# A decoder kernel of two attention calls: the rows of narrow layers' next item normalised by ScalarE, the order of wide layers changed

## The reference, cut to what matters

```python
x = x + _L0_attn_ref(_layernorm(x), ...)      # "window": keys within 32 positions
x = x + _L0_xattn_ref(ctx, ctx, _layernorm(x), padding_mask, ...)   # "cross_pad": 77 context keys
x = x + _L0_ffn_ref(_layernorm(x), ...)       # mixture of 8 experts, the best 2
x = x + _L1_attn_ref(_layernorm(x), ...)      # "causal"
x = x + _L1_xattn_ref(_layernorm(x), ctx, ctx, mask, ...)           # "cross_mask": 77 context keys
x = x + _L1_ffn_ref(_layernorm(x), ...)       # quantised, gated
```

## Time and profile before

| | |
|---|---|
| time, median of 3 runs | 2198.09 us (2197.56 to 2198.1) |
| the profiled execution | 2189.82 us, its span 2188.2 us |
| PE busy | 1992.9 us (91%) |
| DVE busy | 1245.5 us (57%) |
| ACT busy | 965.0 us (44%) |
| POOL busy | 688.6 us (31%) |
| first attention call, in the span | about 0 to 655 us |
| experts | about 655 to 1205 us |
| second attention call | about 1205 to 1851 us |
| feed-forward | about 1856 to 2188 us |

### The profile page before, as it was taken

How to read it: one execution, slowest core, us unless ns; L and a number is a source line. 1 busy time by engine, 2 the same in 40 slices (tenths; PEclk the granted TensorE clock), 3 DMA queues, 4 the chain that set the end, 5 groups by cost and what they waited for, 6 DMA issues and landing times. The chain is left out here.

```text
span 2188.2 us, 51471 instructions
## 1 busy us (share of the span) xinstructions
PE 1992.9 (91%) x17362; PEld 1531.9 (70%) x17362; DVE 1245.5 (57%) x5443; ACT 965.0 (44%) x1849; POOL 688.6 (31%) x1254
## 2 busy tenths in 40 slices
PE   7999998999967999999999799999988887999869
PEld 5777776666646999999998577777666664444357
DVE  5778885566641101111115688888777775459964
ACT  3455555666632333333333255555545553357400
POOL 3566665245561000000001545553422220013400
PEclk9999999999978999999999899999999998999989
DMA  7333332233319999999995644333233321000023
GB/s 216 108 106 108 103 122 86 89 106 111 112 68 359 376 339 346 337 347 336 347 335 190 186 127 135 122 125 108 83 99 97 95 92 43 0 0 1 0 58 96
DMA packets 209108, 334.50 MB, mean 153 GB/s; under 512 B 59453, under 2 KB 193250, under 8 KB 199874
## 3 DMA queue, kind: packets, MB, share of 16 engines
q1 hardware_dynamic: 194482, 301.82, 39.6%
q0 software_dynamic: 9552, 26.10, 3.9%
q10 hardware_dynamic: 4928, 4.72, 0.6%
HBM read 193.74 MB, written 28.05 MB: 101 GB/s over the span
## 5 line engine op out<-in xcount | busy, mean ns | idle before, releaser
L1913 ACT ACTIVATE moe_h<-moe_h_ps,moe_weights 128x128 f32<-128x128 f32 x424 | 132.8, 364 | 254.3 <-PE moe_h_ps L1885 226.0
L2344 PE MATMUL ffn_prod_ps<-x_sb,ffn_weights 128*128 128x512 f32 x480 | 210.9, 599 | 9.7 <-ACT ffn_sig_q L2330 7.0
L1251 ACT ACTIVATE causal_prob<-causal_ps 128x768 f32<-128x768 f32 (+1 forms) x192 | 168.7, 879 | 113.2 <-PE causal_ps L1500 111.8
L1945 DVE TENSOR_TENSOR moe_y<-moe_y_ps,moe_weights 128x256 f32<-128x256 f32 x53 | 22.5, 425 | 328.1 <-PE moe_y_ps L1895 328.1
L1885 PE MATMUL moe_h_ps<-moe_h,moe_weights 128*128 128x128 f32 x1696 | 198.0, 275 | 0.0
L1832 POOL DMA_DIRECT2D moe_y_dram<-moe_y x71 | 39.4, 555 | 494.6 <-DVE moe_y L1945 494.6
L1885 PEld LDWEIGHTS moe_h_ps<-moe_h,moe_weights 128*128 128x128 f32 x1696 | 193.6, 192 | 0.1
L2344 PEld LDWEIGHTS ffn_prod_ps<-x_sb,ffn_weights 128*128 128x128 f32 x480 | 91.0, 192 | 127.2 <-issue 110.2
L984 DVE CUSTOM_DVE_ANT_0 causal_masked<-causal_ps,causal_causal_mask 128x256 bf16<-128x256 f32 (+1 forms) x512 | 152.4, 354 | 45.2 <-PE causal_ps L1466 43.5
L984 DVE CUSTOM_DVE_ANT_0 window_masked<-window_ps,window_window_mask 128x160 bf16<-128x160 f32 x512 | 135.3, 320 | 60.4 <-PE window_ps L1466 57.8
L1251 ACT ACTIVATE window_prob<-window_ps 128x640 f32<-128x640 f32 x128 | 90.0, 703 | 97.7 <-PE window_ps L1500 96.2
(11 more groups left out here) (376 smaller groups left out, 4675.8 us busy)
## 6 DMA issues: line engine op xcount, KB each, us to landing
moe_weights<-moe_w_in SPq DMA_DIRECT2D x53, 2180.0 KB, 9.0
q_pair<-parts SPq DMA_DIRECT2D x512, 128.0 KB
parts<-moe_w_in SPq DMA_DIRECT2D x18, 2180.0 KB, 8.9
k_pair<-parts SPq DMA_DIRECT2D x256, 128.0 KB
k_pair<-parts SPq DMA_DIRECT2D x256, 38.5 KB
moe_rows<-moe_slots_dram SPq DMA_DIRECT2D x71, 128.0 KB, 3.1
moe_y_dram<-moe_y POOLq DMA_DIRECT2D x71, 128.0 KB, 3.4
x_before_ffn_dram<-x_sb SPq DMA_DIRECT2D x16, 256.0 KB, 2.2
```

The source lines that it names most:

```text
L1251: nc.scalar.activation(out, src, ACT.Exp).then_inc(expd, 1)
L1913: nc.scalar.activation(out[:, f, :], psum[:, f // 2, (f % 2) * TM:(f % 2) * TM + TM], ACT.Gelu, bias=bias[:, f:f + 1]).then_inc(done, 1)
L2344: op = nc.tensor.matmul(prod_ps[:, slot, f, :].rearrange("p (b t) -> p b t", b=2), w[:, k, at:at + P], x_cols(n // GROUPS, k), start=(k == ...
```

## The change

Two names are added: wide(ref), true where the layer at lag 2 has two pairs, and by_scalar(ref), true where there is a next item and the layer at lag 2 is narrow.

1. POOL's layernorm makes also a shift, -mean x rstd, by two more 128x2 operations with a semaphore wait before each, for every item; `scaled_by` is raised behind them. It waits for `normed` of t - 1 first.
2. Where by_scalar(ref) holds, DVE's normalise in slot 7 is left out. ACT makes the rows by two ACTIVATEs with scale rstd and bias shift at the end of slot 4, ahead of the copy of v and of max_rows; it waits for `scaled_by` and `xT_mm`.
3. In wide steps PE's turn of xn goes ahead of shifted(0). max_out for the first half of the maxima goes from slot 4 to slot 7, ahead of the output projection, and ACT's max_rows from slot 5 to slot 7. PE's transposes of the output wait for one maximum fewer.
4. The second half of the tail's turn goes to bank 0, like the first, and waits for ACT's copy of the first instead of for `q_lo` and `added`; ACT's copy of it stands at the end of slot 4 and no longer waits for `v_ev`.
5. In DVE's slot 2 the low part of q goes ahead of the last layernorm's statistics.

```diff
@@ attention()
         ln = layernorm_tiles(sb)
+        shift = ln["var_eps"]
+        negative = sb("negative", [P, ST], F32)
+        def wide(ref):
+            return active(ref, 2) and layer_at(ref, 2).pairs == 2
+        def by_scalar(ref):
+            return active(ref, -1) and active(ref, 2) and not wide(ref)
@@ POOL
                 def layernorm(t, ref):
                     pool.wait_ge(stat, t + 1)
-                    inverse_deviation(nc, pool, ln, ref % 2, pool_chain, 1 + t, scaled_by)
+                    par = ref % 2
+                    wait(pool, normed, t - 1)
+                    inverse_deviation(nc, pool, ln, par, pool_chain, 1 + t, deviated)
+                    pool.wait_ge(deviated, t + 1)
+                    nc.gpsimd.tensor_tensor(shift[par][:], ln["mv"][par][:, :, 0], ln["rstd"][par][:], ALU.mult).then_inc(shift_one, 1)
+                    pool.wait_ge(shift_one, t + 1)
+                    nc.gpsimd.tensor_tensor(shift[par][:], shift[par][:], negative[:], ALU.mult).then_inc(scaled_by, 1)
@@ DVE
+                        if i == 2 and active(ref, 0):
+                            low_part(q_parts[par], q_ps, layer_at(ref).bq, q_hi, q_lo, t, S)
                         if i == 2 and in_tail(ref, 4):
...
-                        if i == 2 and active(ref, 0):
-                            low_part(q_parts[par], q_ps, layer_at(ref).bq, q_hi, q_lo, t, S)
@@
-                        if i == 7 and active(ref, -1):
+                        if i == 7 and active(ref, -1) and not by_scalar(ref):
                             dve.wait_ge(scaled_by, t + 2)
@@ ACT
+                def normal_rows(t, ref):
+                    par = ref % 2
+                    act.wait_ge(scaled_by, t + 1)
+                    act.wait_ge(xT_mm, t - 1)
+                    gate(act, act_passed)
+                    for s in range(ST):
+                        op = nc.scalar.activation(xn[par][:, s, :], in_x(t, ref)(t, s), ACT.Identity, bias=shift[par][:, s:s + 1],
+                                                  scale=ln["rstd"][par][:, s:s + 1])
+                    op.then_inc(normed, 1)
@@
-                    if k == 1 and active(ref, 0):
-                        act.wait_ge(v_ev, t + 1)
...
-                    nc.scalar.activation(out, bank(k)[:, S:2 * S], ACT.Copy).then_inc(last_ev, 1)
+                    nc.scalar.activation(out, bank(0)[:, S:2 * S], ACT.Copy).then_inc(last_ev, 1)
@@
-                        if i == 5 and in_tail(ref, 5):
-                            keep_turned(t, ref, 1)
-                        if i == 5 and active(ref, 1):
+                        if i == 5 and active(ref, 1) and not wide(ref):
                             max_rows(t, 1, 0)
@@
+                        if i == 4 and by_scalar(ref):
+                            normal_rows(t + 1, ref + 1)
+                        if i == 4 and in_tail(ref, 5):
+                            keep_turned(t, ref, 1)
+                        if i == 7 and active(ref, 1) and wide(ref):
+                            max_rows(t, 1, 0)
@@ PE
-                        op = nc.tensor.transpose(bank(k)[:, S + s * P:S + s * P + P],
+                        op = nc.tensor.transpose(bank(0)[:, S + s * P:S + s * P + P],
@@
+                        if i == 0 and active(ref, 0) and wide(ref):
+                            turn_normed(t, ref)
...
-                        if i == 0 and active(ref, 0):
-                            pe.wait_ge(normed, t + 1)
...
+                        if i == 0 and active(ref, 0) and not wide(ref):
+                            turn_normed(t, ref)
@@
                         if i == 4 and in_tail(ref, 5):
-                            wait(pe, q_lo, upto(t, ref, 0))
-                            wait(pe, added, upto(t, ref, 4))
+                            pe.wait_ge(last_ev, tail_item(t, 5) * 2 + 1)
+                            if routing(ref, 6) or routing(ref, 7):
+                                pe.wait_ge(seen, tail_item(t, 6) + 1)
                             last_turn(t, ref, 1)
@@
-                        if i == 4 and active(ref, 1):
+                        if i == 4 and active(ref, 1) and not wide(ref):
                             wait(pe, k_lo, self_upto(t, ref, 0))
-                            if in_tail(ref, 5):
-                                pe.wait_ge(last_ev, tail_item(t, 5) * 2 + 1)
@@
-                            wait(pe, m_ev, upto(t, ref, 1, 2) - (1 if active(ref, 1) else 0))
+                            if wide(ref):
+                                wait(pe, m_ev, upto(t, ref, 2, 2))
+                            else:
+                                wait(pe, m_ev, upto(t, ref, 1, 2) - (1 if active(ref, 1) else 0))
@@
                             pe.wait_ge(oT_ev, t - 2)
+                            if active(ref, 1) and wide(ref):
+                                max_out(t, 1, 0)
```

More of the change, by code:

```diff
@@ L300, in attention @@
         scaled_by = sem("scaled_by")
+        deviated = sem("deviated")
+        shift_one = sem("shift_one")
         dve_passed = sem("dve_passed")
@@ L625, in _ @@
                 nc.gpsimd.memset(ln["eps"][:], EPS)
+                nc.gpsimd.memset(negative[:], -1.0)
                 nc.gpsimd.memset(ln["half"][:], -0.5).then_inc(pool_chain, 1)
@@ L1338, in step @@
                             keep_oT(t)
-                        wide = active(ref, 2) and layer_at(ref, 2).pairs == 2
-                        turned_first = wide and (i == 0 and active(ref, 0) or i == 6 and active(ref, 3))
+                        turned_first = wide(ref) and (i == 0 and active(ref, 0) or i == 6 and active(ref, 3))
                         if active(ref, 2) and not turned_first:
@@ L1561, in ranks, with turn_normed @@
                                      skip_group_check=True).then_inc(rank_mm, 1)
+                def turn_normed(t, ref):
+                    par = ref % 2
+                    pe.wait_ge(normed, t + 1)
+                    wait(pe, oT_ev, upto(t, ref, 4))
+                    wait(pe, m_ev, upto(t, ref, 2, 2) - 1)
+                    for k in range(KC):
+                        for s in range(ST):
+                            op = nc.tensor.transpose(xT_ps[:, k, s * P:s * P + P], xn[par][:, s, k * P:k * P + P], ident[:])
+                    op.then_inc(xT_mm, 1)
                 def max_out(t, lag, hf):
@@ L1659, in step @@
                             op.then_inc(v_mm, 1)
-                        if i == 4 and active(ref, 1):
+                        if i == 4 and active(ref, 1) and not wide(ref):
                             wait(pe, k_lo, self_upto(t, ref, 0))
-                            if in_tail(ref, 5):
-                                pe.wait_ge(last_ev, tail_item(t, 5) * 2 + 1)
-                            if routing(ref, 6) or routing(ref, 7):
-                                pe.wait_ge(seen, tail_item(t, 6) + 1)
                             wait(pe, m_ev, upto(t, ref, 2, 2))
```

## The result

The changed kernel takes 2281.42 us (median of 4 runs, 2273.51 to 2286.02) against 2198.03 us: a ratio of 1.0376, 95% interval 1.0347 to 1.0405, so 83 us more. The forecast was 2231 with a range of 2208 to 2268. The direction was right, the size was not, and the time lies in the reach of rival A. The profiled execution took 2273.51 us (span 2271.9), the fastest of the four.

The account below looks back on a forecast made before the run. PE was taken to set every step. Narrow steps lose 48 us and wide steps gain 14.5, so +33.5, taken as 33, on the median of 2198.1 gives 2231 us; range 2208 to 2268.

Parts of the forecast that it names:

- rival A: Window steps: clock also falls to 0.50; 26 us if in half of 16 steps, 51 in all, 2257 to 2282; chance 0.22.
- Part 1: Narrow steps: DVE gives up normalisation, freeing 37 us of DVE beside PE's output projection, worth about 0.
- Part 2: Narrow steps, slot 4: ACT's rows wait for POOL, delaying L1684 by 2.10 us (window) or 0.9 (causal); +48 us.
- Part 3: Wide steps reordered: cross_mask gains 1.1 us per step, 11.5 net; cross_pad 0.35 per step, 3 net; 14.5 us together.
- 14.4 forecast: Causal steps of the second call: 16 steps at 0.9 us more each, 14.4 us.
- The prediction's own sign of being wrong: Forecast is wrong if the clock row of window steps shows less than 1.00.
- the 33.6 forecast: Window steps of the first call: 16 steps at 2.10 us more each, 33.6 us.
- the -3: Cross_pad steps: the new order gains 0.35 us in each of 9 steps, 3 us with ramp and drain.
- The forecast carries 8.3: Whole kernel: median of runs 2198.09 is 8.3 us above the profiled execution's 2189.82, carried along into the forecast time.

Follow-up runs that it names:

- e3: Changed kernel with ACT's rows at the end of slot 7 instead of slot 4: ratio 0.9909 to the kernel before, 2169.0 against 2189.9 us.
- e1: Changed kernel with DVE normalising narrow steps' rows again and ACT doing none of it: ratio 0.9922 to the kernel before, 2173.4 against 2189.9 us.
- e14: Kernel before with only the new order of wide steps, no shift on POOL, no rows on ACT: ratio 0.9915, 2171.5 against 2190.4 us.
- e13: Changed kernel unchanged, timed and profiled once more on another chip: ratio 1.0310 to the kernel before, 2258.0 against 2190.4 us.
- e2: Kernel before with only the narrow part added (POOL's shift, ACT's rows in slot 4), old wide order: ratio 1.0416, 2280.7 against 2189.9 us.
- e11: Kernel before with seven unread ACTIVATEs with scale and bias at the end of slot 4 of window steps, first call: ratio 1.0308, 69 us more.
- e10: Kernel before with six unread ACTIVATEs with scale and bias at the end of slot 4 of window steps, first call: ratio 1.0275, 61 us more.
- e9: Kernel before with five unread ACTIVATEs with scale and bias at the end of slot 4 of window steps, first call: ratio 1.0098, 22 us more.
- e5: Changed kernel with seven unread matrix products on PE in slot 4 of window steps: ratio 1.0213 to the kernel before, 2234.7 against 2188.6 us.
- e6: Kernel before with four unread ACT copies at the end of slot 4 of window steps, first call: ratio 1.0008.
- e8: Kernel before with seven unread ACT copies at the end of slot 4 of window steps, first call: ratio 1.0074.

## Why the prediction was right and wrong

Part 1, DVE's relief at 0: right, shown by e3 against e1.

Part 2, the gap: right in mechanism, and in size in window steps. 2.10 forecast for L1684's delay, 2.32 us of idle measured, and 21.89 us for a window step without a fall of the clock, 2.2 more than before (21.8 us forecast). In causal steps 0.9 forecast; measured 0.53 to 0.89, and 1.06 us of idle at the transposes, of which a little is taken back later in the step. The second call's steps 2 to 17 cost 14.1 us against 14.4 forecast, but some 3.5 of that are falls of the clock in steps 3 and 16; without them it is a quarter less than forecast.

Part 3: cross_mask 1.09 to 1.18 per step, against 1.1; the sum -12.4 against -11.5. Cross_pad was sized too small: 0.58 in e14's steps instead of 0.35; in the first profile the rhythm above hid it, in e13 steps 18 to 30 have -8.1 us.

The step that failed is the choice between the forecast and rival A: the sum has no term for the falls of the clock, so they stood at 0. The rows gave two facts: a fall after two microseconds of thin work (62 to 64), and none at 342 to 346, where PE stood 1.26 us. A gap of 2.1 us lay outside both, and I gave the falls 0.22, as if in some steps at most. (That PE now stands "0.59 at most" holds for the steady steps alone, as the 1.26 shows.) The runs put a fall in 14 or all of the fifteen steps 3 to 17, where the gap is mostly 2.2 to 2.4 us (the changed kernel, e2, e11, e13), behind 1.7 to 1.9 in each of steps 4 to 15 (e10), and behind 1.2 to 1.4 in none of these twelve (e9). By e5 the falls cost about 32 us, some 2 us each. The prediction's own sign of being wrong, a clock below 1.00 in the row of a window step, is what came.

Rival A named the mechanism, and its price was too high: 51 us for all sixteen steps. It took 3.2 us from step 3 of the kernel before against a steady step; but step 3 takes 21.00 us in e1 without a fall, so 1.9 of its 22.89 was the fall's. That A's upper end, 2282, meets the 2281 is luck.

What makes up the rest, in the profiled execution (2273.51): steps 2 to 17 of the first call are 31.7 us above the 33.6 forecast; its steps 18 to 30 are 7.6 above the -3, by the rhythm of the cross_pad steps; the ends have some 3. That is 2231 + 42 = 2273. The +8.9 between the calls is no further term. The forecast carries 8.3 already, from a profiled execution of 2189.82 to a median of 2198.1. In e9 to e11, whose kernels differ from the one before in the window steps alone and whose chip runs that one in 2197.25, the stretch is 10.1 to 10.6 us longer; in e6 to e8, with 2188.64, it is 2.6 to 4.3. So most of it seems to go with the chip; on which chips the first two profiles ran isn't known. The median is 8 us above the profiled execution. The other three have no profile; their mean granted clock was 0.939 to 0.942 against 0.946, so they spent more time at 0.50, but where isn't known. In e13, without the rhythm, the loss is 68 us: 33 and 32, and 3 more.

The range ended at 2268 because it took in half of A; with A as the likeliest case it would have held the time, but in part by A's high price.

## What to carry to other kernels

A new wait on a busy engine has two prices: its length, and what the clock does after it. When the profile shows a length that is survived (1.26 us here) and the change makes one well beyond it, in each of many steps, the fall is the case to forecast and not the exception (here in 14 or 15 of fifteen steps). And before work goes to an engine with idle time, look whether its input is ready in that idle time: the same two instructions cost 91 us in slot 4 (e2) and nothing in slot 7 (e3), or in slot 4 with POOL's order turned round.

## What the runs showed of the hardware

The granted clock has only the two levels 1.00 and 0.50 here, and stays at 0.50 for 3.4, 6.8 or 10.2 us at a time in window steps. The Trainium skill (page TensorE: Matmul & The Clock Gate, section What's actually happening) names the same two levels; the traces agree: no other level stands in any of them.

On ACT a 128x256 copy takes 0.31 us in a row of seven, the same tile with scale and bias from a tile 0.49 us in a row (five to seven in e9 to e11). Products that nobody reads, in a gap, bought 24 us net in the window steps of this kernel, where PE is the bound (e5).
